# Nine words to a row: how TensorE reads its window offsets and range bases while it builds two matrices from an edge list

## The reference

```
h = relu(layernorm(x));  W = zeros(1024, 1024); W[src, dst] += edge_weight
x = x + h @ W.T + bias
h = relu(layernorm(x))
mean(h) = segment_sum(h[src], dst) / max(degree, 1)
g = relu(h @ W_self0 + mean(h) @ W_neigh0 + b0)
out = x + g @ W_self1 + mean(g) @ W_neigh1 + b1
```

## Time and profile before

| | |
|---|---|
| median of 3 runs | 805.71 us (805.12 to 807.25) |
| profiled execution, own time | 804.5 us |
| its span, first to last instruction | 802.6 us |
| TensorE busy | 769.4 us, 96% of the span |
| VectorE, GpSimd, ScalarE busy | 60%, 51%, 46% |
| mean granted TensorE clock | 0.995 |

### The profile page before, as it was taken

How to read it: one execution, slowest core, us unless ns; L and a number is a source line. 1 busy time by engine, 2 the same in 40 slices (tenths; PEclk the granted TensorE clock), 3 DMA queues, 4 the chain that set the end, 5 groups by cost and what they waited for, 6 DMA issues and landing times.

```text
span 802.6 us, 13233 instructions
## 1 busy us (share of the span) xinstructions
PE 769.4 (96%) x4533; PEld 636.9 (79%) x4534; DVE 483.8 (60%) x719; ACT 370.9 (46%) x526; POOL 412.6 (51%) x569
## 2 busy tenths in 40 slices
PE   3877999999999999999999999999999999999998
PEld 2766888888888888888877888888888888887786
DVE  7998477778454889867313342136559766245443
ACT  7866734334354222223246886453223323357663
POOL 5000167567659898765732210137899747624310
PEclk9999999999999999999999999999999999999999
DMA  3122457675666753668845653566745658668654
GB/s 111 42 70 93 124 185 218 227 233 172 216 211 208 257 172 104 198 209 302 272 157 177 210 157 105 171 223 229 256 131 171 211 189 321 232 203 273 208 158 141
DMA packets 83126, 151.38 MB, mean 189 GB/s; under 512 B 10965, under 2 KB 21068, under 8 KB 83056
## 3 DMA queue, kind: packets, MB, share of 16 engines
q1 hardware_dynamic: 61534, 102.65, 40.5%
q10 hardware_dynamic: 20002, 42.91, 15.1%
q0 software_dynamic: 1520, 4.92, 1.5%
HBM read 103.79 MB, written 46.65 MB: 187 GB/s over the span
## 4 chain that ended last, share of the span: by engine, by line
PE 81%; DVE 8%; DMA 4%; POOL 3%; issue 2%; ACT 2%; SPq 0%; POOLq 0%; ACTq 0%; DVEq 0%
PE bank L1436 45%; PE bank L1478 18%; PE bank L1371 12%; DVE L L1660 2%; DVE R L1645 2%; DVE L L1652 1%; PE bank L1283 1%; PE bank L1494 1%; DMA cst<-prod1g_scratch 1%; DMA b<-in_L_gnn_b 1%; PE bank L1267 1%; PE bank L1364 1%; DMA bias<-in_L_gnn_bias 1%; POOL split L922 1%; ACT Ax L1147 1%
## 5 line engine op out<-in xcount | busy, mean ns | idle before, releaser
L1436 PE MATMUL bank<-slot,split 128*128 128x512 f32 x1680 | 386.5, 390 | 0.2 <-POOL split L922 0.2
L1436 PEld LDWEIGHTS bank<-slot,split 128*128 128x128 f32 x1680 | 313.6, 188 | 66.4 <-issue 2.0
L884 POOL TENSOR_TENSOR AT<-AT,az 128x50 int32 (+3 forms) x288 | 96.8, 336 | 118.4 <-DMA az<-asum_scratch 76.6
L922 POOL TENSOR_TENSOR split<-stage,split 128x512 fp32r<-128x512 f32 x50 | 66.0, 1322 | 115.1 <-ACT split L1115 114.8
L1147 ACT CAST Ax<-AT 128x1280 fp32r<-128x1280 uint16 x40 | 107.0, 2678 | 35.1 <-PE bank L1478 28.0
L1795 DVE TENSOR_TENSOR slot<-T,slot 128x512 fp32r<-128x512 f32 x64 | 88.7, 1410 | 22.8 <-ACT slot L1106 21.5
L1371 PE MATMUL bank<-slot,split_m 128*128 128x512 f32 x320 | 91.2, 396 | 0.0
L1915 DVE SCALAR_TENSOR_TENSOR cst<-bank,dinv,stage 128x512 f32<-128x512 f32 x40 | 30.1, 751 | 96.0 <-PE bank L1478 92.5
L1115 ACT CAST split<-stage 128x512 fp32r<-128x512 f32 x50 | 31.1, 625 | 120.5 <-PE bank L1436 68.5
L1478 PE MATMUL bank<-slot,Ax 128*128 128x512 f32 x320 | 77.2, 393 | 0.4 <-ACT Ax L1147 0.4
L939 POOL TENSOR_TENSOR T<-T,wst 128x512 f32<-128x512 f32 x48 | 69.9, 1471 | 5.4 <-DMA wst<-in_L_gnn_W_self 5.3
(11 more groups left out here) (193 smaller groups left out, 1033.0 us busy)
## 6 DMA issues: line engine op xcount, KB each, us to landing
stage<-hT_scratch SPq DMA_DIRECT2D x90, 256.0 KB, 3.6
wst<-in_L_gnn_W_neigh SPq DMA_DIRECT2D x56, 256.0 KB, 4.4
wst<-in_L_gnn_W_self SPq DMA_DIRECT2D x56, 256.0 KB, 3.0
x1b_scratch<-x ACTq DMA_DIRECT2D x10, 512.0 KB, 5.2
hT_scratch<-hTs ACTq DMA_DIRECT2D x10, 512.0 KB, 3.0
stage<-prod0s_scratch SPq DMA_DIRECT2D x20, 256.0 KB, 3.0
hT_scratch<-h1s ACTq DMA_DIRECT2D x20, 256.0 KB, 3.5
stage<-prod1s_scratch SPq DMA_DIRECT2D x20, 256.0 KB, 2.7
```

The costliest lines, as they stand in the source:

```text
L884: pool.tensor_tensor(a, a, az32[:, n % NZ, pairs * pos:pairs * (pos + 1)], ALU.add) \
L922: pool.tensor_tensor(split[:, v % 2, 1, :], source(v), split[:, v % 2, 0, :].bitcast(F32), ALU.subtract).then_inc(s_olo, 1)
L1436: last = pe.matmul(dense_bank(v, which)[:, :], split[:, v % 2, a, NT * k:NT * (k + 1)], slot[t % 2][:, b, HF * (HK * which + k):HF * (HK * ...
```

## The change

The table `tab_o` gets nine words a group: the eight offsets and the base beside them, copied in one DMA from columns 0 to 8 of `tab_g`. That DMA now waits for ScalarE's first signal as well. From group 6 on (`ALONE`, the first group whose chunks each have their own offset) one register load reads three rows of nine, 27 words, from word 9j; group 36 has one row. Groups 0 to 5 read their offsets as before, with rows nine words apart. The four loads of bases, and the wait for `tab_w` before group 3, are gone from TensorE. `s_assert_within` only tells the compiler the bounds of a value. ScalarE goes on reading `tab_w`.

```
-AT_ONCE = 24
-BASES = {3: range(4, 8), 8: range(8, 16), 15: range(16, 32), 31: range(32, LATE)}
+GR = GC + 1
+ALONE = SHARED.index(1)
+ROWS_AT_ONCE = 3
...
-        tab_o = sb("tab_o", [1, NG * GC], I32, build)
+        tab_o = sb("tab_o", [1, NG * GR], I32, build)
...
-            sp.dma_start(tab_o[:, :], tab_g[:, OFFW:OFFW + GC]).then_inc(s_tabo, 16)
+            sp.wait_ge(s_tabg, 1)
+            sp.dma_start(tab_o[:, :], tab_g[:, OFFW:OFFW + GR]).then_inc(s_tabo, 16)
...
             def load_offsets(j):
-                each = GC // SHARED[j]
-                upto = j + 1
-                while upto < LATE and SHARED[upto] == SHARED[j] and each * (upto + 1 - j) <= AT_ONCE:
-                    upto += 1
-                values = load(pe, tab_o[0:1, GC * j:GC * upto:SHARED[j]], 0, (WW - WD) * TW)
-                offsets_of.update((n, values[each * (n - j):each * (n - j + 1)]) for n in range(j, upto))
+                if j < ALONE:
+                    upto = j + SHARED[j:].count(SHARED[j])
+                    each = GC // SHARED[j]
+                    values = load(pe, tab_o[0:1, :].rearrange("p (r c) -> p r c", c=GR)[:, j:upto, 0:GC:SHARED[j]], 0,
+                                  (WW - WD) * TW)
+                    offsets_of.update((n, values[each * (n - j):each * (n - j + 1)]) for n in range(j, upto))
+                    return
+                upto = min(j + ROWS_AT_ONCE, LATE)
+                values = load(pe, tab_o[0:1, GR * j:GR * upto], 0, N)
+                for n in range(j, upto):
+                    row = values[GR * (n - j):GR * (n - j + 1)]
+                    offsets_of[n] = [nc.s_assert_within(v, 0, (WW - WD) * TW, skip_runtime_bounds_check_because=clamped)
+                                     for v in row[0:GC]]
+                    base_of[n] = nc.s_assert_within(row[GC], 0, F, skip_runtime_bounds_check_because=clamped)
...
-                if j in BASES:
-                    if j == 3:
-                        pe.wait_ge(s_tabw, 16)
-                    base_of.update(zip(BASES[j], load(pe, tab_w[0:1, BASES[j].start:BASES[j].stop], 0, F)))
```

## The result

The changed kernel takes 853.97 us (median of 5 runs, 851.66 to 857.13) against 805.19 us before: ratio 1.0593, 95% interval 1.0572 to 1.0613. It is 49 us slower; 850 was predicted, in a range of 830 to 868. The profiled execution has a span of 852.7 us instead of 802.6, +50.1.

What follows compares the result with a forecast made beforehand. TensorE, waiting for its own register loads, was taken to pace the edge stage. The sum 36.1 + 0.5 - 1.6 + 10 = +45 us on 804.5 gave 849.5, so 850 us was predicted, range 830 to 868.

Steps and rivals of the forecast that it cites:

- (a): Groups 6, 9, 15, 18, 21, 27, 30, 33: 27-word loads off the border fetched word by word, 6.36 us each, +36.1 us.
- (b): Loads on the border: a seventh piece at groups 12 and 24, +0.5 us together; group 36's extra piece hidden, uncovered +0.25.
- (c): Base loads gone from TensorE: -0.4 us before group 3, -1.2 before group 15, 0 before groups 8 and 31.
- (d): Edge stage from group 15: longer stops put about half of 22 groups at 1.2 GHz, +13, cover -3; taken +10 us.
- What bounds the stage: Edge stage from group 3 on: TensorE waits for its own register loads, so any growth delays all that follows.
- The pairs of words: Groups 6, 18, 30, two words off: perhaps 14 fetches instead of 27, -9 us, giving the lower end of 830.
- (e): Start of the kernel: the table's DMA also waits for ScalarE's copy, loads of groups 0 to 5 unchanged, 0 us.
- Fours anyway: Rival on the long loads: rows fetched in fours wherever they start, total +0.9 to +2.9 us; chance 0.09.
- only the ends: Rival: off-border loads fetch only end words singly, 9 fetches for 27 words, about +5 us in total; chance 0.04.
- Faster: Rival at groups 3, 8, 15, 31: seventh piece free, four loads less save 1.6 to 3.0 us; chance 0.03.

Runs made afterwards that it cites:

- experiments 1 and 2: The kernel before with only table `tab_o` moved: one word later in 1 (860.11 us, ratio 1.0666), four words later in 2 (806.28 us, ratio 1.0001).
- experiment 5: The changed kernel with each load's start rounded down to a 16-byte border, its end left where it is: 812.49 us, executed once.
- experiment 3: The changed kernel with each load widened at both ends to multiples of four words, extra registers unused: 810.38 us, ratio 1.004 to the kernel before.
- experiment 6: The changed kernel with six long float32 matmuls ahead of each of the eight loads off the border: 845.54 us, ratio 1.0482 to the kernel before.
- experiment 10: The changed kernel with rows of twelve words, one row loaded before each group, all on borders: 806.63 us, ratio 1.0013 to the kernel before.

## Why the prediction was right

The number was right by its mechanism: eight loads fetched word by word, in front of TensorE, and a slower clock behind them. By the turning of W the sum was 45 and 49.05 was measured; the 4 us are +2.0 in (a), +1.2 in (b), -0.5 in (c) and +1.4 in (d).

**What bounds the stage.** It was read from a wait that the trace put down to "R" and to "issue" while a register load stood in the queue. In the changed kernel the first matmul of a group comes 0.1 to 0.2 us after the end of its long load, and the stage moves by what the loads take.

**(a), the eight loads.** Predicted +36.1, measured 52.9 - 14.8 = +38.1. The price per word was 0.243 us, (6.61 - 0.54) / 25, instead of 0.233. The step that decided, that a row off the border is fetched word by word, was an inference from rows on the border alone; experiments 1 and 2 show it with nothing else changed. The pairs of words that the lower end of the range allowed for, in rows two words off, didn't come: group 6 took 6.51 us. The Trainium skill's 200 ns a register ("Runtime: NRT & Kernel Launch", section "Instruction fetch mechanics") is near the 0.24 us of rows off the border, and three times too high for those on it (1.62 us for 24 words is 0.07 each).

**(b), the loads on the border.** Mis-sized: +0.25 each was predicted, +0.75 and +0.97 measured. Seven fetches were counted for 27 words, but the three words of the end cost a fetch each; experiment 5 has it. +1.7 in all instead of +0.5.

**(c), the bases.** -0.4 before group 3: its first matmul is at 18.63 instead of 19.05. The load of 1.11 us before group 15 is gone, -1.2. The one before group 8 had been put at nothing because no idle time followed it, and that was wrong: from the first matmul of group 6 (23.17) to the start of group 9's load (27.6) the kernel before takes 4.4 to 4.5 us with it, and the changed kernel 4.0 without (27.64 to 31.6), as experiments 3 and 5 do. So it cost 0.5 of its 0.78 us. Work that delays the next load costs time although TensorE never stands still behind it. In the same way the one before group 31 cost some 0.15 (experiment 3 has 4.43 us where the kernel before has 4.58). In all -2.1 instead of -1.6.

**(d), the clock.** Predicted +10. 49.05 - 38.1 - 1.7 + 2.1 leaves 11.4 for it. The timeline has it by place: from the first matmul of a set of three groups to the start of the next load the changed kernel takes 0.6 and 0.3 us more than the kernel before behind the loads of groups 12 and 15, 1.8 behind each of 18 and 21, nothing behind 24, and 2.2 to 2.4 behind each of 27, 30 and 33, some 11.3 together. With TensorE kept busy, 8 to 9 us come back (8.67 by the turning of W); the rest doesn't, and experiment 6 too has a granted clock of 0.83 between 30 and 60 us. Two parts of the estimate were off and made up for each other, which is luck. A group of 340 columns at 1.2 GHz takes 2.96 us, where 3.4 had been scaled from the narrower ones, and 1.73 at full clock, since the 1.88 of group 31 held the load of bases. And the 3 us that longer cover was to give back were 0.6: TensorE's work after the start of a load lasted as long as before, within 0.2 us, at six of the eight loads, and longer only before groups 9 and 21 (by 0.3 and 0.6 us). That "most of the stage has 2.4" GHz rests on the clock column, which says nothing before 33.4 us.

**(e)** The first register load and the first matmul of group 0 come as before (12.23, and 12.26 before), so the second signal that the table's DMA waits for costs nothing.

**The rivals.** *Fours anyway* and *only the ends* fall with experiment 1: by the second, 24 words one word off would be 9 fetches and some 2.4 us, and they took 5.88. The second was right about ends, but only for rows whose start is on the border: off it nothing is fetched in fours. *Faster* falls with the result; had each row been on a border, the change would have cost nothing (experiment 10) or 3.5 us (experiment 3), and won nothing.

## What to carry to other kernels

Where a register load stands in an engine's queue, read its duration before you believe the semaphore that a wait is put down to. Lay tables that are loaded into registers out in multiples of four words from a 16-byte border, and pad rows to that: 27 words off the border cost 6.5 to 6.9 us, 28 on it 1.9 to 2.3. And load little before each use rather than much before every third, so that the work already queued hides more of it.

## What the runs showed of the hardware

- A register load of TensorE costs an estimated 0.11 us and about 0.25 us a fetch, and up to 0.4 more for reasons that stay open. A fetch brings four words if the load's words lie in a row and begin on a 16-byte border, else one. A load that begins on a border but ends inside a piece pays for the last one to three words singly, so that 27 words (2.36 us) cost more than 28 (1.87).
- How far off the border a row begins makes no difference: 6.50 us one word off (group 9), 6.51 two (group 6), 6.63 three (group 15).
- Stops of 5.3 to 6.2 us before every three groups brought the granted clock down to 0.65 to 0.77 from 60 us on, where the kernel before has 1.00, for 8 to 11 us on top of the stops themselves. Six long matmuls beside each load got 8 to 9 us back; twenty short ones lost 18 us more, with loads that started 0.45 us after the first of them instead of before TensorE ran dry.
- A register load can cost time though no idle time follows it: one of 0.78 us before group 8 moved the next load by 0.5 us.
